# First attention: values transposed by DMA in two fp16 parts, in place of TensorE products with the identity

## What is computed

```python
q = (layernorm(x) @ Wq).reshape(b, 128, 16, 128) / sqrt(128)
k = (ctx @ Wk).reshape(b, 2048, 16, 128)
v = (ctx @ Wv).reshape(b, 2048, 16, 128)
attn = softmax(einsum('bqhd,bkhd->bhqk', q, k))
x = x + einsum('bhqk,bkhd->bqhd', attn, v).reshape(b, 128, 2048) @ Wo
```

## Time and profile before

| | |
|---|---|
| median of three runs | 748.55 us |
| the profiled execution | 750.32 us, its span 749.0 us |
| TensorE busy | 670.9 us, 90% |
| VectorE busy | 575.8 us, 77% |
| ScalarE busy | 371.3 us, 50% |
| GpSimd busy | 198.6 us, 27% |
| mean granted clock of TensorE | 0.958 |
| first attention | from 22 to 498 us of the span |

### The profile page before, as it was taken

How to read it: one execution, slowest core, us unless ns; L and a number is a source line. 1 busy time by engine, 2 the same in 40 slices (tenths; PEclk the granted TensorE clock), 3 DMA queues, 4 the chain that set the end, 5 groups by cost and what they waited for, 6 DMA issues and landing times. The chain is left out here.

```text
span 749.0 us, 13021 instructions
## 1 busy us (share of the span) xinstructions
PE 670.9 (90%) x4894; PEld 426.0 (57%) x4894; DVE 575.8 (77%) x1069; ACT 371.3 (50%) x584; POOL 198.6 (27%) x315
## 2 busy tenths in 40 slices
PE   4899999999999999799899999979998988879743
PEld 3456676667666767476566667744553444334431
DVE  3698876977776787677687776749989999999555
ACT  4553334333433443253334336318868998778711
POOL 3285333343334301240000000016324332223100
PEclk9999999999999999899999999989999999999855
DMA  8456965555555578566366475637977999888900
GB/s 285 122 136 145 205 135 126 129 122 118 124 130 122 119 152 232 115 177 167 84 143 182 115 142 131 151 139 136 187 144 142 189 198 177 141 131 158 171 1 7
DMA packets 330639, 107.29 MB, mean 143 GB/s; under 512 B 297032, under 2 KB 328016, under 8 KB 330320
## 3 DMA queue, kind: packets, MB, share of 16 engines
q1 hardware_dynamic: 330576, 106.45, 66.6%
HBM read 32.23 MB, written 0.26 MB: 43 GB/s over the span
## 5 line engine op out<-in xcount | busy, mean ns | idle before, releaser
L804 PE MATMUL psum<-c_nat,eT 128*128 128x256 f16 x1536 | 190.7, 275 | 0.0
L1487 ACT ACTIVATE cT<-psum,bias,q_scale 128x1024 f16<-128x1024 f32 x128 | 153.5, 1203 | 39.7 <-PE psum L1412 33.7
L778 PE MATMUL psum<-cT,qk 128*128 128x512 f16 x768 | 171.0, 379 | 1.2 <-ACT cT L715 1.1
L804 PEld LDWEIGHTS psum<-c_nat,eT 128*128 128x128 f16 x1536 | 152.0, 99 | 26.5 <-issue 0.3
L1412 PE MATMUL psum<-kT,v_space 128*128 128x512 f16 x512 | 144.5, 391 | 20.1 <-DVE tops L1518 15.9
L1518 DVE TENSOR_REDUCE tops<-psum 128x1 f32<-128x512 f32 x256 | 158.1, 679 | 2.4 <-PE psum L1412 2.2
L778 PEld LDWEIGHTS psum<-cT,qk 128*128 128x128 f16 x768 | 74.9, 98 | 86.1 <-ACT cT L715 1.3
L927 DVE TENSOR_REDUCE neg_max<-psum 128x1 f32<-128x2048 f32 x32 | 73.3, 2290 | 33.3 <-PE psum L778 33.1
L1412 PEld LDWEIGHTS psum<-kT,v_space 128*128 128x128 f16 x512 | 45.6, 99 | 91.5 <-DVE tops L1518 61.9
L915 DVE TENSOR_TENSOR e_lo<-e_all,e_hi 128x2048 f16<-128x2048 f32 x32 | 77.5, 2422 | 0.0
L890 ACT ACTIVATE e_all<-psum,neg_max 128x2048 f32<-128x2048 f32 x32 | 63.1, 1973 | 11.3 <-DVE neg_max L929 11.3
(11 more groups left out here) (224 smaller groups left out, 796.2 us busy)
## 6 DMA issues: line engine op xcount, KB each, us to landing
wq_h<-in_L_xattn_Wq SPq DMA_DIRECT2D x32, 128.0 KB, 2.2
wk_h<-in_wkT SPq DMA_DIRECT2D x32, 128.0 KB, 2.2
wv_h<-in_L_xattn_Wv SPq DMA_DIRECT2D x32, 128.0 KB, 2.2
wo_h<-in_L_xattn_Wo SPq DMA_DIRECT2D x32, 128.0 KB, 2.2
mx_land<-in_mx_weights SPq DMA_DIRECT2D x8, 384.0 KB, 3.5
v_space<-in_ctx SPq DMA_DIRECT2D x4, 512.0 KB, 7.4
cT<-in_ctx SPq DMA_DIRECT2D x2, 1024.0 KB, 11.1
c_nat<-in_expert_wT SPq DMA_DIRECT2D x2, 1024.0 KB, 5.9
```

What stands on the lines that cost most here:

```text
L778: ins = pe.matmul(s_ps[:, n * 512:(n + 1) * 512], c.qk[:, u % 2, q_part, k, :], m.cT[:, b, c_part, 4 * n:4 * n + 4, k, :], start=(k, q_par ...
L804: ins = pe.matmul(u_ps, c.eT[:, v % 2, e_part, j, :], m.c_nat[:, v // H0, c_part, j, :], start=(j, e_part, c_part) == (0, 0, 0), stop=(j, ...
L1487: act.activation(x.y[:, u % 2, q * CHUNK:(q + 1) * CHUNK], m.bank(3 + 2 * (q % 2), 2), ACT.Exp, bias=x.bias[:, u:u + 1], scale=m.q_scale[: ...
```

## The change

For the first 30 of the 32 units (`TURNED`), u no longer goes through TensorE. ScalarE writes u's high part in fp16 (`u_parts[:, 0]`), VectorE reads the same PSUM again and writes the rest in fp16 (`u_parts[:, 1]`), right ahead of `remainder`. SP transposes both parts in one DMA, issued between those of e_hi and e_lo, and GpSimd adds the transposed parts into `uT_sb`. The last two units go the old way. VectorE's reciprocal comes earlier in the round. GpSimd's steps of the mixer, the experts and the queries, which ran behind all key tiles, are now run in its rounds, behind that round's add. The mixer's transpose xT moves from place (19, 2) to (19, 3). The bank of the products' result is waited for ahead of L837 in place of L819.

```diff
+TURNED = UNITS - 2
...
-MIX_AT = dict(norm=(18, 2), again=(18, 3), scaled=(19, 0), plus=(19, 1), xT=(19, 2), qkv0=(20, 0), qkv1=(20, 2),
+MIX_AT = dict(norm=(18, 2), again=(18, 3), scaled=(19, 0), plus=(19, 1), xT=(19, 3), qkv0=(20, 0), qkv1=(20, 2),
...
             sp.dma_start_transpose(c.eT[:, v % 2, 0], c.e_hi[:, :]).then_inc(s[f"hi_turned{v % 2}"], 16)
+            sp_turn_values(sp, c, s, v - 2)
             sp.wait_ge(s["e_lo"], v + 1)
...
+def sp_turn_values(sp, c, s, v):
+    if 0 <= v < TURNED:
+        if v > 0:
+            sp.wait_ge(s["uT_out"], v)
+        sp.wait_ge(s["u_lo"], v + 1)
+        sp.dma_start_transpose(c.uT_parts.rearrange("p a k q -> p (a k) q"), flat(c.u_parts)).then_inc(
+            s[f"u_turned{v % 2}"], 16)
...
-    for u in range(H0):
+    for u in range(UNITS + 3):
+        w = u - 3
+        if 0 <= w < TURNED:
+            pool.wait_ge(s[f"u_turned{w % 2}"], 16 * (w // 2 + 1))
+            if w > 0:
+                pool.wait_ge(s["oT"], w)
+            pool.tensor_tensor(flat(c.uT_sb), flat(c.uT_parts[:, 0]), flat(c.uT_parts[:, 1]), ALU.add).then_inc(
+                s["uT_out"], 1)
+        side.upto(4 * u + 3)
...
-                pe.wait_ge(s["u_out"], v)
+                pe.wait_ge(*read_values(s, v - 1))
...
-        if w >= 0:
-            pe.wait_ge(s["u_out"], w + 1)
-            if w > 0:
-                pe.wait_ge(s["added"], w)
+        if w >= TURNED:
+            pe.wait_ge(s["u_out"], w - TURNED + 1)
+            pe.wait_ge(s["added"], w)
             for k in range(KD):
                 ins = pe.transpose(o_ps[:, k * P:(k + 1) * P], c.u_sb[:, k * P:(k + 1) * P], m.ident[:, :])
...
+                act.mul(c.u_parts[:, 0, :], u_ps, c.inv_sum[:, :]).then_inc(s["u_hi"], 1)
...
         side.upto(4 * u + 3)
+        if 0 <= v < TURNED:
+            dve.wait_ge(s["u_hi"], v + 1)
+            dve.scalar_tensor_tensor(c.u_parts[:, 1, :], u_ps, c.inv_sum[:, :], c.u_parts[:, 0, :], ALU.mult,
+                                     ALU.subtract).then_inc(s["u_lo"], 1)
```

More of the change, by code:

```diff
@@ L73 @@
     late_hi late_lo late_turned
-    scores raw_max max exp e_hi e_lo hi_turned0 hi_turned1 lo_turned0 lo_turned1 pv inv_sum u_out uT uT_out oT oT_out
+    scores raw_max max exp e_hi e_lo hi_turned0 hi_turned1 lo_turned0 lo_turned1 pv inv_sum u_out u_hi u_lo u_turned0 u_turned1 uT uT_out oT oT_out
     head_out added
@@ L278, in __init__ @@
         self.u_sb = sb("u_sb", [P, D])
+        self.u_parts = sb("u_parts", [P, 2, D], FP16)
+        self.uT_parts = sb("uT_parts", [P, 2, KD, P], FP16)
         self.uT_sb = sb("uT_sb", [P, KD, P])
@@ L607, in pool_constants, with pool_cross @@
                            ALU.subtract).then_inc(s["c_lo_pool"], 1)
-def pool_cross(pool, m, c, d, s):
+def pool_cross(pool, m, c, d, s, side):
     full = d.k_full.rearrange("p (h d) -> p h d", h=H1)
-    for u in range(H0):
+    for u in range(UNITS + 3):
[7 more added lines that the diff above has]
+        side.upto(4 * u + 3)
         if u in (1, 2):
@@ L617, in pool_cross @@
                                ALU.subtract).then_inc(s["late_lo"], 1)
-        for kt in (2 * u, 2 * u + 1):
+        for kt in (2 * u, 2 * u + 1) if u < H0 else ():
             ints = d.k_int[:, kt % 2, :].rearrange("p (h d) -> p h d", h=H1)
@@ L630, in pool_cross @@
             pool.tensor_tensor(lo, full, hi, ALU.subtract).then_inc(s["k_cut"], 1)
+    side.rest()
 def pe_query(pe, m, c, s, u):
@@ L759, in dve_setup, with read_values @@
                              ALU.mult, ALU.subtract).then_inc(s["wkv_lo"], 1)
+def read_values(s, v):
+    return (s["u_lo"], v + 1) if v < TURNED else (s["u_out"], v - TURNED + 1)
 def pe_cross(pe, m, c, d, g, s, side):
@@ L870, in act_cross @@
         side.upto(4 * u)
[L871 to L874, removed]
+        if w >= TURNED:
+            act.wait_ge(s["uT"], w - TURNED + 1)
+            act.wait_ge(s["oT"], w)
             act.copy(flat(c.uT_sb), o_ps[:, 0:D]).then_inc(s["uT_out"], 1)
@@ L901, in act_cross @@
             act.wait_ge(s["inv_sum"], v + 1)
-            if v > 0:
-                act.wait_ge(s["uT"], v)
-            act.mul(c.u_sb[:, :], u_ps, c.inv_sum[:, :]).then_inc(s["u_out"], 1)
+            if v < TURNED:
+                if v > 0:
+                    act.wait_ge(s[f"u_turned{(v - 1) % 2}"], 16 * ((v - 1) // 2 + 1))
+                act.mul(c.u_parts[:, 0, :], u_ps, c.inv_sum[:, :]).then_inc(s["u_hi"], 1)
+            else:
+                if v > TURNED:
+                    act.wait_ge(s["uT"], v - TURNED)
+                act.mul(c.u_sb[:, :], u_ps, c.inv_sum[:, :]).then_inc(s["u_out"], 1)
         side.upto(4 * u + 3)
 def dve_cross(dve, m, c, d, g, s, side):
-    s_ps, kv_ps, o_ps = m.bank(0, 4), m.bank(5), m.bank(6)
+    s_ps, kv_ps, o_ps, u_ps = m.bank(0, 4), m.bank(5), m.bank(6), m.bank(7)[:, 0:D]
     def remainder(v):
@@ L946, in dve_cross @@
             dve.tensor_tensor(m.x_res[:, b, :], m.x_res[:, b, :], o_ps[:, 0:D], ALU.add).then_inc(s["added"], 1)
+        if 0 <= v < UNITS:
+            if v > 0:
+                dve.wait_ge(*read_values(s, v - 1))
+            dve.wait_ge(s["exp"], v + 1)
+            dve.reciprocal(c.inv_sum[:, :], c.row_sum[:, v:v + 1]).then_inc(s["inv_sum"], 1)
         if u < H0:
@@ L950, in dve_cross @@
             dve_fold_key(dve, m, c, s, u + 2)
[L951 to L955, removed]
         side.upto(4 * u + 2)
@@ L1902, in perceiver @@
                                                dve_queries(dve, m, s, 0, room, queries)))
-            pool_cross(pool, m, c, d, s)
-            Side(pool_mix(pool, m, x, s, 0, mix), pool_experts(pool, m, s, 0, experts),
-                 pool_queries(pool, m, s, 0, queries)).rest()
+            pool_cross(pool, m, c, d, s, Side(pool_mix(pool, m, x, s, 0, mix), pool_experts(pool, m, s, 0, experts),
+                                              pool_queries(pool, m, s, 0, queries)))
             sp_cross(sp, m, c, d, g, s, t)
```

## The result

The changed kernel takes **765.78 us** (median of 4 runs, 763.99 to 767.04), the kernel before 748.63 (4 runs, 746.19 to 753.58): a ratio of 1.022, 95% interval 1.016 to 1.028. The prediction was 753.4 us, with a range of 745 to 761. Slower was right; the loss is 17 us where 4.9 were forecast. The profiled executions took 767.04 and 750.32 us, their spans are 765.7 and 749.0: 16.7 us to explain.

The account below looks back on a forecast made before the run. The prediction took the first attention as bound by TensorE. Its terms, −5.1 + 5.8 + 2.4 + 0.8 − 2.3 + 0.4 + 0.4 + 2.5 = +4.9 us on the median 748.55, gave 753.4 us, range 745 to 761.

Parts of the forecast that it names:

- the gain per round: In 23 of rounds 3 to 32, each pair of identity products removed from TensorE saves 0.22 us: −5.1 us.
- the cover in the rounds 5 to 16: The add of the transposed values ends before TensorE asks, with 1.6 us to spare in round 6.
- round 4: Two large context transposes hold SP, so the values come late: +5.8 us, and +2.4 for the clock behind the wait.
- Rival B: Faster: the transpose is hidden in round 4 too, as the large transposes don't keep SP; 744.0 us, chance 0.14.
- the price of nothing for what stands behind SP's new wait: e_lo's transpose, the keys' transposes and the weights' loads on SP are not wanted before the next round; no cost.
- The term for round 17: VectorE is late, e_lo arrives 0.4 later and the diagonals 0.8 later: +0.8 us (0 to 1.8).
- the term for rounds 23 and 26: VectorE's chains come 0.1 and 0.3 later and the 0.22 isn't gained: +0.4 us (0 to 0.9).
- round 19: The add ends at 301.5, but xm's later turn removes TensorE's old wait: −2.3 us (−4.0 to −1.0 by the clock).
- round 32: No scores cover the chain; e_hi holds SP and the add ends at 485.3, against 482.41: +2.5 us (2.0 to 4.1).
- 31: Round 31: values added at 475.2, against 474.81: +0.4 us (0 to 3 with neighbours 29 and 30).
- A: Not slower: TensorE keeps its full clock through the waits of rounds 4 and 19; 749.3 us, chance 0.27.
- C: Much slower: every transfer lands at 4.1 us instead of 2.5; 763.9 us, chance 0.08.

Follow-up runs that it names:

- Run 1: Changed kernel with the two large context transposes issued one each behind the keys' transposes of rounds 4 and 5; 757.07 us.
- run 2: Changed kernel with the load of the next weights' slice issued right behind the high part of the exponentials instead of last in the round; 764.1 us.
- run 6: Changed kernel without VectorE's low part from head 14 on, SP waiting for the high part, transpose and add kept; 764.61 us.
- run 9: Kernel before with the slice's load early and xT one place later, no value transposed by DMA; 741.45 us.
- run 4: Kernel before with the slice's load issued right behind the high part of the exponentials; 744.89 us.
- run 7: Run 1's kernel with the eight loads of the mixer's weights moved on SP from the end of round 18 to that of 17; 758.08 us.
- run 10: Run 1's kernel with 29 heads on the new way in place of 30, so round 32 uses the products with the identity; 751.85 us.
- run 3: Changed kernel with only the first 14 heads on the new way, the others by the products with the identity; 753.97 us.
- run 5: Run 3's kernel with VectorE also writing the low part for the 16 heads from 14 on, nothing using it; 756.72 us.
- run 8: Changed kernel with only the first 14 heads on the new way, the large transposes moved and the slice's load early; 740.66 us.

## Why the prediction was right or wrong

*Right: the gain per round.* The 23 rounds gave 5.0 us for 5.1, and the cover in the rounds 5 to 16 held. The seven rounds in which it would fail were also named; elsewhere nothing was lost.

*Right: round 4*, +7.1 for 8.2. The wait was 5.70 us for 5.8; the clock behind it was priced a little high, 1.4 for 2.4 (granted 0.75 from 85.24 to 91.00). Run 1 shows the cause. Rival B fell with it.

*Wrong, the step that failed: the price of nothing for what stands behind SP's new wait* ("none of them wanted before the next round"). VectorE does want one of them in the same round: the load of the weights' slice. (The term for round 17 even counted 0.4 us for one such load; no other term did.) The waits of VectorE by releaser (us in all, times, the longest), from 262 to 500 us, before and after:

```profile
DVE mx_amax L1012 <- DMA mx_land<-in_mx_weights: 17.8, 8, 3.2
```

```profile
DVE mx_amax L1048 <- DMA mx_land<-in_mx_weights: 22.2, 8, 4.3
```

In round 26, SP and VectorE before:

```profile
405.79 0.58 SPq L558 DMA_DIRECT2D mx_land<-in_mx_weights  x1
...
409.25 0.95 DVE L1012 TENSOR_REDUCE mx_amax<-mx_land 128x24 f32<-128x768 f32 x1 [2.56 <-DMA mx_land<-in_mx_weights]
```

and after:

```profile
415.63 0.58 SPq L562 DMA_DIRECT2D mx_land<-in_mx_weights  x1
...
418.99 0.95 DVE L1048 TENSOR_REDUCE mx_amax<-mx_land 128x24 f32<-128x768 f32 x1 [3.50 <-DMA mx_land<-in_mx_weights]
```

TensorE was 8.8 us behind at that point, the load is 9.84 later: 1 us more. VectorE passes it on to x_res, TensorE's wait grows from 2.12 to 3.28, and now the clock falls as well. That is the term for rounds 23 and 26, +0.4, which came to 5.5; run 2, with the load early, took it away. In round 26 it is the queue and not VectorE's low part that makes the load late: in run 6, without that part, VectorE still waits 3.63 us for it. Round 17 lost 1.3 us more than forecast in the same way: the first slice's load, behind the keys' transposes, came late, and VectorE waited 2.44 us for it instead of 1.34.

*Wrong: round 19* (+2.4 for −2.3). xT's move did what was said: no wait for xm is left, and run 9 against run 4 shows what the move alone is worth. The add came 3.5 us later than reckoned. SP's queue and GpSimd in the changed kernel:

```profile
300.38 5.56 SPq L541 DMA_TRANSPOSE eT<-e_hi  x1
306.04 1.20 SPq L592 DMA_TRANSPOSE uT_parts<-u_parts  x1
```

```profile
310.02 0.92 POOL L631 TENSOR_TENSOR uT_sb<-uT_parts 128x256 f32<-128x256 f16 x1 [6.14 <-DMA uT_parts<-u_parts]
```

With TensorE 5.9 us behind, the working meant e_hi at 299.6 and the transpose's issue at 304.3. It came at 306.04, because the queue of round 18 was longer by a transpose, and e_hi held SP for 5.56 us instead of 4.65; then it took 4.0 us to land, not 2.5. The low clock behind the wait cost 2.9 us (granted 0.64 from 310.99 to 319.00) where 1.7 were reckoned. The failed step is again the queue, reckoned as if only VectorE's 0.4 us moved it.

*Wrong by size: round 32* (+6.0 for +2.5) *and 31* (+2.1 for +0.4). In 32 the transfer took 3.9 us in place of 2.5, and the low clock behind the wait another 1.7, which no term held. Of the thirty transfers four took 4 us, in the rounds 19, 22, 26 and 32; the median was right, and three of the four fell into rounds priced one by one. The same rounds are slow in the runs 1, 6, 7 and 10 (3.6 to 4.2 us; in 10 round 32 goes the old way), so it is their place and not chance; what about the place stays open.

Ahead of round 31 VectorE again waits longer for the load, here the last slice's; before and after:

```profile
467.68 0.95 DVE L1012 TENSOR_REDUCE mx_amax<-mx_land 128x24 f32<-128x768 f32 x1 [3.24 <-DMA mx_land<-in_mx_weights]
```

```profile
480.90 0.95 DVE L1048 TENSOR_REDUCE mx_amax<-mx_land 128x24 f32<-128x768 f32 x1 [4.35 <-DMA mx_land<-in_mx_weights]
```

In run 2, with the load early, round 31 loses nothing; but round 30 does there, so this isn't a clean test.

*The rivals.* A's point, that the clock holds if round 19's idle time is cut in pieces, did not come: it was cut (1.35 and 5.73 us), and the clock fell. C came nearest in time, 763.9, but not by its mechanism: most transfers landed in 2.4.

*The rule of the Trainium skill*, TensorE where the result may go to PSUM (VectorE: DVE Perf Modes, "Rules for kernel authors"), spoke against the change, and the change is slower. The 1309 ns a square that the Trainium skill gives for the DMA path (the same page, "The three transpose paths"), an estimate of 5.2 us for four, isn't what the change's transfers took (2.4 in the median, 4.2 at most): the rule came out right here by the queue and not by that figure.

*Not forecast: −3.3 us after 518 us.* Most of it is one wait of the second attention; TensorE before, and the same product after:

```profile
705.05 0.56 PE L1439 MATMUL psum<-v_space,c_nat 128*128 128x16 f16 x16 [2.51 <-DMA c_nat<-cT]
```

```profile
721.46 0.56 PE L1475 MATMUL psum<-v_space,c_nat 128*128 128x16 f16 x16
```

The wait (2.4 to 2.7 us) is there in the runs 3, 4, 5, 8 and 9, and missing in all with 29 or 30 heads on the new way. Why is open.

## What to carry to other kernels

A step that moves work off the bound engine onto an in-order DMA queue must be priced for everything issued behind it in that round: write down, for each later transfer, who waits for it and when. A wait that a trace of before already shows for such a transfer (17.8 us here) means that it has no slack: a later issue is a later VectorE. Moving that transfer to an earlier place, in the kernel before, gained 3.7 us, where the change lost 17. Run the control without the new path before crediting it with a faster version.

## What the runs showed of the hardware that was not expected

Whether the clock falls behind an idle time doesn't follow from its length alone. Stretches behind TensorE's waits (us, busy us of PE, PEld, DVE, ACT, POOL, granted clock, DMA share, GB/s), in the changed kernel behind 5.73, 3.28 and 3.50 us of idle:

```profile
311.00:314.50 3.50, 3.50 (x16) 2.75 (x17) 2.12 (x2) 2.23 (x3) 3.34 (x4) 0.50 0.13 28
423.20:429.80 6.60, 6.56 (x18) 3.55 (x19) 1.69 (x5) 0.00 (x0) 0.00 (x0) 0.53 0.10 27
500.60:505.00 4.40, 4.38 (x24) 3.35 (x25) 0.00 (x0) 0.27 (x1) 0.00 (x0) 0.61 0.36 74
```

In run 3 behind 3.71 us, and in run 2 behind 2.05:

```profile
368.90:372.30 3.40, 3.40 (x29) 3.03 (x30) 0.73 (x3) 0.74 (x2) 0.00 (x0) 1.00 0.27 77
```

```profile
472.10:476.00 3.90, 3.82 (x19) 2.89 (x20) 0.82 (x6) 2.81 (x4) 0.03 (x1) 0.56 0.46 93
```

Up to the wait TensorE had worked without a pause at a granted clock of 1.00 in both (busy 15.1 of 15.1 us from 350.00 in run 3, 20.1 of 20.1 from 450.00 in run 2). The longer idle time left the 2.4 GHz level alone, the shorter one brought the 1.2 GHz level. The granted clock of 0.53 for 6.6 us in round 26 cost about 3 us, more than the 1.16 us by which the wait had grown.
